# A gated cross-attention and mixture block: full-row down matmuls for the small unit, and five steps in another order

## The chip, the cores and the metric

The kernel runs on one core of a Trainium2 chip. The metric is the device time of one execution in microseconds (us). The engines are TensorE (PE in the profile; PEld are its weight loads), VectorE (DVE), ScalarE (ACT), GpSimd (POOL) and SyncE (SP), which issues the transfers.

## The reference, cut to what matters

```python
# 4 batches of 256 tokens, D = 256; per 128-wide block: scale to 448, round to fp8, scale back
x = x + tanh(g_xattn) * einsum(quant_act(layernorm(x)), quant_weight(ctx))      # per batch
h = layernorm(x)
comb = top-4 of softmax(h @ gate_w.T), made to sum to 1                         # 8 experts
moe  = sum_e comb[:, e] * ((silu(h @ wg[e].T) * (h @ wu[e].T)) @ wd[e].T)       # 176 rows each
sh   = (silu(h @ swg.T) * (h @ swu.T)) @ swd.T                                  # 704 rows
x = x + tanh(g_ffn) * (moe + sigmoid(h @ shared_gate_w.T) * sh)
```

## The kernel before, in words

**Units.** The 8 experts' 176 rows and the shared 704 make 2112 weight rows, cut into 17 units of 128 rows (`UNITS`). Units 0 to 5 of a pass are the shared part, and the last of these, position 5, has only 64 rows (`LAST`, `is_small`). Units 6 to 16 are the experts. The 1024 tokens go in two halves of 512 (batches 0 and 1, then 2 and 3), so that `n` runs from 0 to 33.

**A unit.** Products are kept near fp32 by splitting each operand into a high part, rounded to fp32r, and a low rest. ACT writes the high part of a unit's gate and up weights (`high_gu`), of its down weights (`high_d`) and of the activations (`high_a`), and applies silu (`silu_unit`). POOL writes the low parts of the weights (`low_gu`, `low_d`), DVE multiplies silu by up (`gated`), by the routing weight (`mixed`) and makes the low activations (`low_a`). PE then does `gate(n)` and `up(n)`, 6 matmuls each of 128 rows by 512 tokens, and `down(n - 2)`, 6 more (`three_passes`, L971). The small unit has gate and up side by side in one weight tile, so it has no `up`. Its down weights lie twice in 128 rows, and its activations are stacked: rows 0 to 63 of `a_hi` are the high part and rows 64 to 127 the low. For each half of the columns `down` does two matmuls for it: `d_hi` on 128 rows (L1034) and `d_lo` on 64 (L1035).

**Before the units.** Each batch goes through: variance (DVE), `centre`, `scale_x`, `mags_x` (ACT), `lift_x`, `round_x` (DVE), `transpose_xq` (PE), `copy_xqt` (ACT). Its context goes through `scale_ctx`, `mags_ctx` (ACT), `lift_ctx`, `round_ctx` (DVE). Then come `attend` (PE), `residual0` (ACT), `residual1` and `residual_sum` (DVE), the second layernorm (`stats_x1`, a power on POOL, `shift_x1` on DVE, `norm_x1` on ACT), `transpose_y2` (PE), `high_h` (ACT) and `low_h` (DVE). The block maxima of the context are transposed and spread over the partitions by two small matmuls of 8 rows (`ctx_scale_rows`, L890), which `copy_scales_ctx` reads on DVE; `scale_ctx` waits for that copy.

**Order.** Each engine works its own queue in the order in which the program text has it, with semaphores between the engines. There is no planner. Batches 0 and 1 run before the units. The steps of batches 2 and 3 are written by hand between units 0 to 16, on each engine under its own `if n == ...`. Units 0 and 1 go by batch on PE while batch 1 is still in its second norm: `gate_up_first(n, part)` does 8 matmuls with the high tokens (L1010, L1011; 256 tokens each), waits for `h_lo`, and does 4 with the low ones (L1015). Order there: units 0 and 1 on batch 0, `transpose_y2(1)`, units 0 and 1 on batch 1.

**Routing.** `router` and `transpose_logits` (PE) give the logits of a half, DVE ranks and weighs them, `transpose_comb` (PE, L964) turns the weights, `copy_comb` (ACT, L433) writes `comb_rows`, and SP sends these to DRAM and back, spread over partitions, into `mixw`; `mixed` reads it from unit 6 on.

Of the kernel before, what the change touches and what calls it, by code (L numbers as in the profile page):

```python
# [20 lines left out]
UNITS = FULL + 1  # L21
# [58 lines left out]
def flamingo_gated_block(nc, xs, ctx_t, small, w_full, w_last, comb_d, out_t):  # L80
    with ExitStack() as stack:
# [210 lines left out]
        def _(pool):  # L292
# [25 lines left out]
            def low_d(n):  # L318
                c, slot, rows = CHUNKS[n % UNITS], n % DEEP, rows_of(n)
                at = GUL if is_small(n) else GU  # L320
                pool.wait_ge(d_hi_done, n + 1)
                nc.gpsimd.tensor_tensor(d_lo[0:rows, slot, :], w_raw[0:rows, c, at:at + D],  # L322
                                        d_hi[0:rows, slot, :].bitcast(F32), ALU.subtract).then_inc(d_lo_done, 1)
# [33 lines left out]
        def _(a):  # L357
# [86 lines left out]
            def high_d(n):  # L444
                c, slot, rows = CHUNKS[n % UNITS], n % DEEP, rows_of(n)
                at = GUL if is_small(n) else GU
                rows = 2 * LAST if is_small(n) else rows
                nc.scalar.activation(d_hi[0:rows, slot, :], w_raw[0:rows, c, at:at + D], ACT.Copy).then_inc(d_hi_done, 1)  # L448
# [21 lines left out]
            high_gu(0)  # L470
# [9 lines left out]
            mags_x(1)  # L480
            residual0(0)
            high_gu(1)
            copy_xqt(1)
# [68 lines left out]
        def _(v):  # L552
# [231 lines left out]
            lifted = lift_x(0)  # L784
            round_x(0, lifted)
            lifted = lift_ctx(0)
            max_x_1 = max_x(1)
            round_ctx(0, lifted)
            scales_x(1, max_x_1)
            dequant_scales(0)  # L790
            lifted = lift_ctx(1)
            round_ctx(1, lifted)
            lifted = lift_x(1)
            round_x(1, lifted)
# [6 lines left out]
            stats_x1(1)  # L801
            low_h(0)
            shift_x1(1)
# [6 lines left out]
            for n in range(ALL):  # L810
# [68 lines left out]
        def _(pe):  # L879
# [123 lines left out]
            def gate_up_first(n, part):  # L1003
                cols = slice(part * S, (part + 1) * S)
                banks, x_of = (GATE_FIRST[n][:, cols], UP[n][:, cols]), tokens(0, part)
                pe.wait_ge(gu_lo_done, n + 1)
                pe.wait_ge(h_hi_done, part + 1)
                for which, out in enumerate(banks):
                    for k, (hi, lo) in enumerate(w_gu(n, which)):
                        nc.tensor.matmul(out, hi, x_of[k][0], start=(k == 0), stop=False)  # L1010
                        nc.tensor.matmul(out, lo, x_of[k][0], start=False, stop=False)  # L1011
                pe.wait_ge(h_lo_done, part + 1)
# [133 lines left out]
```

## Time and profile before

| | us |
|---|---|
| median of 3 runs | 185.72 (185.38 to 185.96) |
| the profiled execution, its whole time | 185.49 |
| its span | 183.5 |
| PE busy, 723 matmuls | 159.0 (87%) |
| DVE busy | 131.4 (72%) |
| ACT busy | 103.1 (56%) |
| POOL busy | 92.7 (51%) |

The busy time of an engine is the time in which the profile shows an instruction on it; that includes time in which an instruction that has begun is held back. The granted clock of PE was 1.00 of full speed in every stretch. A matmul's end is modelled; the distance between the starts of two matmuls is the surer number.

### The profile page before, as it was taken

To read this page: it belongs to the slowest core of one execution; us is meant where nothing else is said; L and a number is where in the kernel's file an instruction comes from. 1 tells how busy PE (TensorE), PEld (TensorE's weight loads), DVE (VectorE), ACT (ScalarE), POOL (GpSimd) and SP (SyncE) were. 2 spreads that over 40 slices of the span, in tenths; PEclk is the share of its full clock that TensorE was granted. 3 is DMA by queue.
4 is the path that set the end of the run, shared out by engine and by line. 5 is a ranking of instruction groups with operands and counts; after the bars stand their busy time and mean duration, and the time that the engine had idled before them with its cause. 6 is when DMAs were issued, how large, how long until landed. Compare 5 with 4: busy or idle time off the path is not lost.

```text
span 183.5 us, 2313 instructions
## 1 busy us (share of the span) xinstructions
PE 159.0 (87%) x723; PEld 122.7 (67%) x723; DVE 131.4 (72%) x265; ACT 103.1 (56%) x229; POOL 92.7 (51%) x92
## 2 busy tenths in 40 slices
PE   0022688999889999999997999999999999999992
PEld 0010357877568688777885887887886888888871
DVE  1878984897998999999866962977278455444463
ACT  2499563958546886474746764445654554443430
POOL 3120615653744468556317995556545555553450
PEclk9999999999999999999999999999999999999999
DMA  5999992000019940000000000200299400000003
GB/s 140 289 404 340 321 311 86 5 0 0 0 61 272 255 103 4 2 2 0 4 0 0 2 0 0 92 25 0 66 251 269 105 4 0 2 0 0 4 0 114
DMA packets 8049, 16.19 MB, mean 88 GB/s; under 512 B 1235, under 2 KB 1235, under 8 KB 8037
## 3 DMA queue, kind: packets, MB, share of 16 engines
q1 hardware_dynamic: 8036, 16.04, 28.9%
q8 instruction: 6, 0.10, 0.2%
q14 instruction: 7, 0.05, 0.1%
HBM read 14.95 MB, written 1.09 MB: 87 GB/s over the span
## 4 chain that ended last, share of the span: by engine, by line
PE 68%; DVE 14%; ACT 10%; issue 3%; DMA 2%; POOL 0%; DVEq 0%
PE bank L971 58%; ACT xc L380 2%; DMA x<-xs 2%; DVE act L737 2%; DVE x L660 2%; PE bank L923 2%; ACT xc L409 2%; DVE a_lo L753 1%; PE bank L1010 1%; ACT cw L372 1%; DVE bn L571 1%; ACT silu L457 1%; PE bank L1015 1%; PE bank L1011 1%; DVE amax_x L615 1%
## 5 line engine op out<-in xcount | busy, mean ns | idle before, releaser
L315 POOL TENSOR_TENSOR gu_lo<-w_raw,gu_hi 128x512 fp32r<-128x512 f32 (+1 forms) x34 | 47.5, 1398 | 21.6 <-ACT gu_hi L442 13.4
L322 POOL TENSOR_TENSOR d_lo<-w_raw,d_hi 128x256 fp32r<-128x256 f32 (+1 forms) x34 | 32.6, 960 | 44.1 <-ACT d_hi L448 44.0
L971 PE MATMUL bank<-h_hi,gu_hi 128*128 128x512 f32 x124 | 49.6, 400 | 0.5 <-ACT silu L457 0.4
L971 PE MATMUL bank<-h_hi,gu_lo 128*128 128x512 f32 x124 | 49.2, 397 | 0.0
L971 PE MATMUL bank<-h_lo,gu_hi 128*128 128x512 f32 x124 | 49.1, 396 | 0.0
L457 ACT ACTIVATE silu<-bank 128x512 f32<-128x512 f32 (+1 forms) x34 | 20.2, 594 | 45.8 <-PE bank L971 44.7
L747 DVE TENSOR_TENSOR act<-silu,mixw 128x512 f32<-128x512 f32 x18 | 14.7, 814 | 22.0 <-ACT silu L457 22.0
L753 DVE TENSOR_TENSOR a_lo<-act,a_hi 128x512 fp32r<-128x512 f32 x32 | 28.1, 877 | 0.7 <-ACT a_hi L465 0.7
L971 PEld LDWEIGHTS bank<-h_hi,gu_hi 128*128 128x128 f32 x124 | 23.3, 188 | 6.9 <-issue 1.6
L971 PEld LDWEIGHTS bank<-h_hi,gu_lo 128*128 128x128 f32 x124 | 23.3, 188 | 5.5
L971 PEld LDWEIGHTS bank<-h_lo,gu_hi 128*128 128x128 f32 x124 | 23.4, 189 | 5.2
L971 PE MATMUL bank<-a_hi,d_hi 128*128 128x512 f32 x62 | 25.2, 406 | 0.0
L971 PE MATMUL bank<-a_lo,d_hi 128*128 128x512 f32 x62 | 24.3, 392 | 0.0
L971 PE MATMUL bank<-a_hi,d_lo 128*128 128x512 f32 x62 | 24.3, 392 | 0.0
L465 ACT ACTIVATE a_hi<-act 128x512 fp32r<-128x512 f32 (+1 forms) x34 | 21.2, 623 | 5.5 <-DVE act L737 4.8
L737 DVE TENSOR_TENSOR act<-silu,bank 128x512 f32<-128x512 f32 (+1 forms) x16 | 11.0, 686 | 14.0 <-PE bank L971 10.2
L442 ACT ACTIVATE gu_hi<-w_raw 128x512 fp32r<-128x512 f32 (+1 forms) x34 | 20.8, 613 | 0.1
L308 POOL TENSOR_TENSOR rstd<-ve,minus_half 128x2 f32<-128x2 f32 x8 | 5.9, 740 | 18.9 <-DVE ve L581 18.8
L448 ACT ACTIVATE d_hi<-w_raw 128x256 fp32r<-128x256 f32 x34 | 13.8, 406 | 0.0
L971 PEld LDWEIGHTS bank<-a_hi,d_hi 128*128 128x128 f32 x62 | 11.6, 188 | 2.8 <-issue 0.3
L971 PEld LDWEIGHTS bank<-a_hi,d_lo 128*128 128x128 f32 x62 | 11.6, 188 | 2.6
L971 PEld LDWEIGHTS bank<-a_lo,d_hi 128*128 128x128 f32 x62 | 11.7, 188 | 2.4
(117 smaller groups left out, 194.8 us busy)
## 6 DMA issues: line engine op xcount, KB each, us to landing
w_raw<-w_full SPq DMA_DIRECT2D x16, 384.0 KB, 5.2
mixw<-comb_d SPq DMA_DIRECT2D x10, 256.0 KB, 5.7
x<-xs SPq DMA_DIRECT2D x4, 256.0 KB, 6.4
cw<-ctx_t SPq DMA_DIRECT2D x4, 256.0 KB, 5.8
out_t<-fin SPq DMA_DIRECT2D x4, 256.0 KB, 2.3
mixw<-comb_d SPq DMA_DIRECT2D x4, 224.0 KB, 5.6
mixw<-comb_d SPq DMA_DIRECT2D x4, 192.0 KB, 5.5
mixw<-comb_d SPq DMA_DIRECT2D x4, 160.0 KB, 4.9
```

The costliest lines, as they stand in the source:

```text
L308: nc.gpsimd.tensor_tensor(rstd[:, which, tile_slice(b)], ve[:, which, tile_slice(b)], minus_half[:, 0:BT], ALU.pow).then_inc(rstd_sem, 1)
L315: nc.gpsimd.tensor_tensor(gu_lo[:, slot, 0:cols], w_raw[:, c, 0:cols], gu_hi[:, slot, 0:cols].bitcast(F32), ALU.subtract).then_inc(gu_lo_d ...
L322: nc.gpsimd.tensor_tensor(d_lo[0:rows, slot, :], w_raw[0:rows, c, at:at + D], d_hi[0:rows, slot, :].bitcast(F32), ALU.subtract).then_inc(d ...
L380: last = nc.scalar.activation(xc[:, j, k, :], xc[:, j, k, :], ACT.Copy, scale=mul_x[:, j, k:k + 1])
L442: nc.scalar.activation(gu_hi[:, slot, 0:cols], w_raw[:, c, 0:cols], ACT.Copy).then_inc(gu_hi_done, 1)
L448: nc.scalar.activation(d_hi[0:rows, slot, :], w_raw[0:rows, c, at:at + D], ACT.Copy).then_inc(d_hi_done, 1)
L457: nc.scalar.activation(silu[0:rows, slot, :], src[0:rows, :], ACT.Silu).then_inc(silu_done, 1)
L465: nc.scalar.activation(a_hi[0:rows, slot, :], act[0:rows, slot, :], ACT.Copy).then_inc(a_hi_done, 1)
L737: nc.vector.tensor_tensor(act[0:rows, slot, :], factor[0:rows, slot, :], up, ALU.mult).then_inc(gated_done, 1)
L747: nc.vector.tensor_tensor(act[:, slot, :], factor[:, slot, :], mixw[:, c, :], ALU.mult).then_inc(mixed_done, 1)
L753: nc.vector.tensor_tensor(low, act[0:rows, slot, :], a_hi[0:rows, slot, :].bitcast(F32), ALU.subtract).then_inc(a_lo_done, 1)
L971: last = nc.tensor.matmul(out, w[k][a], x_of[k][b], start=(start and k == 0 and i == 0), stop=(stop and k == blocks - 1 and i == 2))
```

## The change

The small unit's low down weights are made on all 128 rows, and its down matmuls read all 128 rows of `d_hi`, `d_lo` and `a_hi`; the second now also adds the product of the low weights with the low activations. `high_gu(0)` and `high_gu(1)` move back on ACT. `shift_x1(1)` goes ahead of `low_h(0)` on DVE. `gate_up_first` is cut in two, `first_high` (its 8 matmuls with the high tokens) and `first_low` (its 4 with the low ones), and `transpose_y2(1)` stands between these for unit 1, batch 0. `transpose_comb` goes on PE from behind `down` of one iteration to behind the small unit's `gate` of the next, in both halves, and `copy_comb` on ACT from ahead of that unit's silu to behind it. `ctx_scale_rows(1)` goes from n = 5 to between gate(6) and up(6), and the copy of its result on DVE from n = 5 to n = 6, behind `round_x(2)`. Some names are changed and nothing else.

```diff
             def low_d(n):                                     # GpSimd
-                nc.gpsimd.tensor_tensor(d_lo[0:rows, slot, :], w_raw[0:rows, c, at:at + D], ...
+                nc.gpsimd.tensor_tensor(d_lo[:, slot, :], w_raw[:, c, at:at + D], ...
...
             mags_x(0)                                         # ScalarE
-            high_gu(0)
             scale_ctx(0)
...
             mags_x(1)
+            high_gu(0)
             residual0(0)
+            copy_xqt(1)
             high_gu(1)
-            copy_xqt(1)
             residual0(1)
...
                 if n < ALL - 2:
                     high_gu(n + 2)
-                if n == 5:
-                    copy_comb(0)
-                if n == UNITS + 5:
-                    copy_comb(1)
                 if n == ALL - 1:
                     high_a(n - 1)
                 silu_unit(n)
+                if n % UNITS == 5:
+                    copy_comb(n // UNITS)
...
             stats_x1(1)                                       # VectorE
+            shift_x1(1)
             low_h(0)
-            shift_x1(1)
...
                 if n == 5:
-                    copy_scales_ctx(1)
                     scales_x(3, max_x_3)
                     lifted_2 = lift_x(2)
                 if n == 6:
                     round_x(2, lifted_2)
+                    copy_scales_ctx(1)
...
                     if is_small(n):                           # TensorE, in down(n)
-                        nc.tensor.matmul(out[k][:], d_hi[0:2 * LAST, slot, ks], a_hi[0:2 * LAST, slot, :], ...
-                        last = nc.tensor.matmul(out[k][:], d_lo[0:rows, slot, ks], a_hi[0:rows, slot, :], ...
+                        nc.tensor.matmul(out[k][:], d_hi[:, slot, ks], a_hi[:, slot, :], ...
+                        last = nc.tensor.matmul(out[k][:], d_lo[:, slot, ks], a_hi[:, slot, :], ...
...
             keep_clock_up(2)                                  # TensorE
-            gate_up_first(0, 0)
-            gate_up_first(1, 0)
+            first_high(0, 0)
+            first_low(0, 0)
+            first_high(1, 0)
             transpose_y2(1)
-            gate_up_first(0, 1)
-            gate_up_first(1, 1)
+            first_low(1, 0)
+            first_high(0, 1)
+            first_low(0, 1)
+            first_high(1, 1)
+            first_low(1, 1)
...
                 gate(n)
                 if n == 2:
                     transpose_logits(0)
+                if n % UNITS == SHARED_UNITS - 1:
+                    transpose_comb(n // UNITS)
+                if n == 6:
+                    ctx_scale_rows(1)
                 if not is_small(n):
                     up(n)
...
-                if n == 5:
-                    ctx_scale_rows(1)
...
                 down(n - LAG)
-                if n % UNITS == SHARED_UNITS - 2:
-                    transpose_comb(n // UNITS)
```

## Rows read from the trace of the kernel before

**Rows 1.** Busy time by stretch: length, PE, PEld, DVE, ACT, POOL, clock, DMA, GB/s
```profile
64.00:86.00 22.00, 22.00 (x103) 17.36 (x103) 21.95 (x32) 14.38 (x33) 14.12 (x11) 1.00 0.10 26
86.00:100.00 14.00, 13.07 (x61) 10.21 (x59) 9.72 (x26) 8.10 (x19) 5.53 (x7) 1.00 0.00 1
```

**Rows 2.** Chain of work that ended last: start, length, what; its last long piece
```profile
139.39 39.33 PE bank L971 x168
```

**Rows 3.** PE's waits: total us, times, the longest
```profile
PE bank L890 <- DVE diag L594: 2.0, 2, 1.3
PE bank L1010 <- ACT h_hi L420: 1.1, 2, 0.8
PE bank L964 <- DVE comb L725: 0.9, 1, 0.9
```

**Rows 4.** Timeline, 0 to 20 us: start, length, instruction [idle before it]
```profile
9.84 0.17 DVE L599 COPY scl_c<-bank 128x16 f32<-128x16 f32 x1
...
10.07 0.61 ACT L442 ACTIVATE gu_hi<-w_raw 128x512 fp32r<-128x512 f32 x1
...
10.59 1.26 ACT L372 ACTIVATE cw<-cw,scl_c 128x128 f32<-128x128 f32 x4
...
12.55 0.69 DVE L604 SCALAR_TENSOR_TENSOR cw<-cm,cw 128x512 f32<-128x512 bf16 x1 [0.79 <-ACT cm L385]
```

**Rows 5.** Timeline, 20 to 36 us
```profile
25.37 0.70 POOL L308 TENSOR_TENSOR rstd<-ve,minus_half 128x2 f32<-128x2 f32 x1 [2.34 <-DVE ve L581]
...
25.86 0.69 DVE L684 TENSOR_TENSOR h_lo<-bank,h_hi 128x512 fp32r<-128x512 f32 x1 [0.57 <-ACT h_hi L420]
...
26.47 0.15 DVE L678 SCALAR_TENSOR_TENSOR shift<-mv,rstd 128x2 f32<-128x2 f32 x1
...
27.00 0.64 PE L1015 MATMUL bank<-h_lo,gu_hi 128*128 128x256 f32 x4
...
28.90 0.60 PE L923 MATMUL bank<-eye,xc 128*128 128x128 f32 x4
...
29.54 0.60 ACT L420 ACTIVATE h_hi<-bank 128x512 fp32r<-128x512 f32 x1 [1.78 <-PE bank L923]
```

**Rows 6.** Timeline, 49.4 to 66 us, without the weight loads
```profile
50.64 0.68 DVE L753 TENSOR_TENSOR a_lo<-act,a_hi 128x512 fp32r<-128x512 f32 x1
...
52.32 0.39 PE L890 MATMUL bank<-diag,ones 8*128 8x16 f32 x2 [0.73 <-DVE diag L594]
...
57.05 1.27 ACT L372 ACTIVATE cw<-cw,scl_c 128x128 f32<-128x128 f32 x4
...
57.20 0.69 DVE L737 TENSOR_TENSOR act<-silu,bank 128x512 f32<-128x512 f32 x1 [0.53 <-PE bank L971]
...
58.64 0.69 DVE L638 SCALAR_TENSOR_TENSOR xq<-xm,xc 128x512 bf16<-128x512 bf16 x1
...
59.24 1.78 DVE L747 TENSOR_TENSOR act<-act,mixw 128x512 f32<-128x512 f32 x1
...
59.91 0.60 ACT L457 ACTIVATE silu<-bank 128x512 f32<-128x512 f32 x1 [1.07 <-PE bank L971]
...
61.38 0.69 DVE L737 TENSOR_TENSOR act<-silu,bank 128x512 f32<-128x512 f32 x1 [0.35 <-PE bank L971]
```

**Rows 7.** Timeline of the full stage, 75 to 105 us
```profile
82.15 0.97 DVE L610 SCALAR_TENSOR_TENSOR cq<-cm,cw 128x512 bf16<-128x512 bf16 x1
...
83.41 0.61 PE L916 MATMUL bank<-cq,xqt 128*128 128x256 bf16 x4
...
87.49 0.69 DVE L747 TENSOR_TENSOR act<-silu,mixw 128x512 f32<-128x512 f32 x1 [0.28 <-ACT silu L457]
```

**Rows 8.** Timeline of the small unit's down, first half: first matmul, and the next unit's first
```profile
61.32 0.47 PE L1034 MATMUL bank<-a_hi,d_hi 128*128 128x512 f32 x1
...
63.00 0.50 PE L971 MATMUL bank<-h_hi,gu_hi 128*128 128x512 f32 x1
```

**Rows 9.** Groups of instructions with shapes kept apart: total us, mean ns | idle before
```profile
L322 POOL TENSOR_TENSOR d_lo<-w_raw,d_hi 128x256 fp32r<-128x256 f32 x32 | 30.5, 954 | 38.2 <-ACT d_hi L448 38.1
...
L322 POOL TENSOR_TENSOR d_lo<-w_raw,d_hi 64x256 fp32r<-64x256 f32 x2 | 2.1, 1042 | 5.9 <-ACT d_hi L448 5.9
```

More of the change, by code:

```diff
@@ L318, in low_d @@
             def low_d(n):
[L319 removed]
+                c, slot = CHUNKS[n % UNITS], n % DEEP
                 at = GUL if is_small(n) else GU
                 pool.wait_ge(d_hi_done, n + 1)
[L322 to L323 removed]
+                nc.gpsimd.tensor_tensor(d_lo[:, slot, :], w_raw[:, c, at:at + D], d_hi[:, slot, :].bitcast(F32),
+                                        ALU.subtract).then_inc(d_lo_done, 1)
             def add_shared(h, k):
@@ L444, in high_d @@
             def high_d(n):
-                c, slot, rows = CHUNKS[n % UNITS], n % DEEP, rows_of(n)
+                c, slot = CHUNKS[n % UNITS], n % DEEP
                 at = GUL if is_small(n) else GU
-                rows = 2 * LAST if is_small(n) else rows
-                nc.scalar.activation(d_hi[0:rows, slot, :], w_raw[0:rows, c, at:at + D], ACT.Copy).then_inc(d_hi_done, 1)
+                nc.scalar.activation(d_hi[:, slot, :], w_raw[:, c, at:at + D], ACT.Copy).then_inc(d_hi_done, 1)
             def silu_unit(n):
@@ L783, in _ @@
             stats(0, 1, summed_1).then_inc(var_ready, 1)
-            lifted = lift_x(0)
-            round_x(0, lifted)
-            lifted = lift_ctx(0)
+            lifted_x0 = lift_x(0)
+            round_x(0, lifted_x0)
+            lifted_c0 = lift_ctx(0)
             max_x_1 = max_x(1)
-            round_ctx(0, lifted)
+            round_ctx(0, lifted_c0)
             scales_x(1, max_x_1)
             dequant_scales(0)
[L791 to L794, printed above, removed]
+            lifted_c1 = lift_ctx(1)
+            round_ctx(1, lifted_c1)
+            lifted_x1 = lift_x(1)
+            round_x(1, lifted_x1)
             residual1(0)
@@ L1001, in up, with first_banks, first_high @@
                 three_passes(UP[n % 2][:], w_gu(n % SPLIT, 1), tokens(n // UNITS), True, True).then_inc(products_done, 1)
-            def gate_up_first(n, part):
+            def first_banks(n, part):
                 cols = slice(part * S, (part + 1) * S)
-                banks, x_of = (GATE_FIRST[n][:, cols], UP[n][:, cols]), tokens(0, part)
+                return GATE_FIRST[n][:, cols], UP[n][:, cols]
+            def first_high(n, part):
+                x_of = tokens(0, part)
                 pe.wait_ge(gu_lo_done, n + 1)
                 pe.wait_ge(h_hi_done, part + 1)
-                for which, out in enumerate(banks):
+                for which, out in enumerate(first_banks(n, part)):
                     for k, (hi, lo) in enumerate(w_gu(n, which)):
@@ L1011, in gate_up_first, with first_low @@
                         nc.tensor.matmul(out, lo, x_of[k][0], start=False, stop=False)
+            def first_low(n, part):
+                x_of = tokens(0, part)
                 pe.wait_ge(h_lo_done, part + 1)
-                for which, out in enumerate(banks):
+                for which, out in enumerate(first_banks(n, part)):
                     for k, (hi, lo) in enumerate(w_gu(n, which)):
@@ L1019, in down @@
             def down(n):
-                slot, rows, pos = n % DEEP, rows_of(n), n % UNITS
+                slot, pos = n % DEEP, n % UNITS
                 start, stop = pos in (0, SHARED_UNITS), pos in (SMALL_AT, UNITS - 1)
@@ L1033, in down @@
                     if is_small(n):
-                        nc.tensor.matmul(out[k][:], d_hi[0:2 * LAST, slot, ks], a_hi[0:2 * LAST, slot, :], start=False, stop=False)
-                        last = nc.tensor.matmul(out[k][:], d_lo[0:rows, slot, ks], a_hi[0:rows, slot, :], start=False, stop=True)
+                        nc.tensor.matmul(out[k][:], d_hi[:, slot, ks], a_hi[:, slot, :], start=False, stop=False)
+                        last = nc.tensor.matmul(out[k][:], d_lo[:, slot, ks], a_hi[:, slot, :], start=False, stop=True)
                     else:
```

## The prediction

> **What bounds the kernel now.** I read the busy shares by stage first, then TensorE's (PE's) waits, then the timeline at each place of the diff. From 64 us on PE works almost without a gap: 22.00 of 22 us between 64 and 86 us, 13.07 of 14 between 86 and 100 [rows 1], and from 139.39 us the chain of waits is 168 matmuls in 39.33 us, 0.234 us each [rows 2]. So a microsecond taken off the path before some place reaches the end, unless another engine holds it back in between. One does: VectorE (DVE) is busy 21.95 of 22 us between 64 and 86 us [rows 1]. That stage matters most here, as it lies behind nearly all the edits. Before it PE really waits at a few places, and the diff touches three: 0.8 us for h_hi, 0.9 us for comb, and (2.0 less the start-up's 1.3) 0.7 us for the context scales [rows 3].
>
> **1. Context scaled ahead of weights.** The chain at the start runs through ScalarE (ACT). high_gu(0) starts at 10.07 and the context scaling behind it at 10.59, so 0.52 us goes off ACT's queue [rows 4]. Is something else late then? The scales that scale_ctx(0) needs are copied at 9.84 + 0.17 = 10.01 us, 0.06 us ahead of the new start at 10.07. DVE stood idle 0.79 us for the magnitudes of this context before its lift at 12.55 [rows 4], so it moves by the whole 0.52 too and brings the scales and codes of batch 1 with it. high_gu(0) goes to behind mags_x(1): it delays residual0(0), which keeps its old time, while residual1(0) on DVE ends later than it. high_gu(1) goes behind copy_xqt(1), into the time in which ACT waits for PE's attention of batch 1. GpSimd (POOL) reads gu_hi(0) only after the second xq, and takes gu_lo(1) only after x1 of batch 0, so its work is not late by more than it gains. Gain 0.52; bounds 0 and 0.61 (the instruction's own length).
>
> **2. Batch 1's shift ahead of low_h(0).** The variance root of batch 1 ends at 25.37 + 0.70 = 26.07, while its shift starts at 26.47 because low_h(0) at 25.86 is in front [rows 5]. New order: shift at 26.1, normalisation 0.37 us earlier; low_h(0) starts at about 26.17 and ends at 26.86, 0.14 us before the low passes at 27.00 want it [rows 5]. By itself it gives nothing on the path, and costs nothing. If the low passes did wait, it would cost up to 0.3.
>
> **3. Batch 1's transposes between the passes.** They start at 28.90, behind four low passes (0.48 us from the chain's 0.12 a piece: 27.00 to 27.48 for the like group), and h_hi follows at 29.54; PE then stands 0.8 us [rows 3, 5]. Placed ahead of those four passes they start at 28.42, one microsecond after their input is there; h_hi moves from 29.54 to 29.07 and the four passes fill a part of PE's wait. Gain 0.47; bounds 0 and the wait of 0.8. What is late next is h_hi itself: about 0.3 us of the wait stays.
>
> So the kernel is 0.99 us ahead at 34 us. Until 49 us the path alternates between PE, the routing steps on DVE and back, all started by PE, and I let the 0.99 pass. The times below are the old ones, with this 0.99 still to be taken off.
>
> **4. Comb and scale steps later on PE.** Now gate(5) (6 matmuls, 1.4 us by rows 2) runs in the 0.9 us in which PE waited for comb [rows 3], and the transposes find comb ready. Then comes down(3), which needs a_lo(3): DVE makes it at 50.64 + 0.68 = 51.32 [rows 6]. That is a new wait of 1.0 us, where before down(3) came behind the scale matmuls at 52.32 and thus at 52.6. So PE gains 1.3 at down(3). The two scale matmuls now stand in a dense stream between gate(6) and up(6); they took 0.32 us with PE idle ahead of them, here I say 0.4. up(6) and all behind it on PE is 0.8 to 0.9 earlier, and so is gated(6), which waited for it at 57.20 [rows 6]. copy_comb goes behind silu(5): comb_rows is 0.4 later (in these times), against a broadcast that DVE reads first at 59.24; in the second half it is some 1.5 us later, by gate(22) and a silu. There the consumers on PE come two units later (over 4 us), so nothing.
>
> The other side is copy_scales_ctx(1), now behind round_x(2) on DVE, 58.64 + 0.69 = 59.3, or 58.6 with the 0.8 that gated(6) gained. ACT's scale_ctx(2) started at 57.05, and now waits until 58.6: 1.5 us. Behind it in ACT's queue stand high_gu(9) and silu(7): 58.6 + 1.2 + 0.52 gives silu(7) at 60.3 instead of 59.91 [rows 4, 6]. DVE waits for it and does gated(7) at 60.95, 0.4 before its old 61.38 [rows 6], though PE is 1.3 ahead. For this wait DVE had a cover: mixed(6) took 1.78 us at 59.24 where other such products take 0.7, until POOL's low_gu(9) was done. high_gu(9) being late, POOL is idle then and the 1.1 us are saved, to be partly lost in low_a(6), which will meet low_gu(9). I come to 0.3 us for DVE on entering its full stage, bounded by 1.3 (all that PE has) and by a loss of 1.1 (the saved collision comes back at another place). ACT's own 1.5 us of wait is no such bound, since ACT stood idle 1.07 us ahead of silu(7) [rows 6].
> The Trainium skill, page "SBUF — State Buffer", section "SBUF: two separate sides", says that VectorE with two SBUF inputs and GpSimd lock each other out for whole instructions, the first to start winning; the 1.78 us agree with it.
>
> **5. The full stage.** attend(3) on PE at 83.41 needs round_ctx(3), done at 82.15 + 0.97 = 83.12, a slack of 0.29; mixed(13) on DVE at 87.49 waited 0.28 for a silu [rows 7]. With DVE 0.3 earlier and PE more than that, this place comes 0.3 + 0.28, some 0.5 us earlier, and the rest of PE's lead (with the first small unit's saving) is lost in waiting. From here the chain of batch 3's second norm goes to 99.99 us unchanged. Term: 0.5.
>
> **6. Down matmuls of the small unit on all rows.** From 61.32 to 63.00 us four matmuls take 1.68, 0.42 each, where full ones follow at 0.234 [rows 2, 8]. Two have 64 rows and two 128, and all four are slow, so it is the change of rows that costs, some 0.19 each: 0.75 a half, and 0.1 more at the next matmul: 0.8. In the first half it falls before the full stage of DVE (nothing more than term 5). In the second half PE alone is the path: 0.8. Bounds 0 and 0.85. POOL's d_lo on 128 rows instead of 64 costs nothing: on 64 rows it took 1042 ns mean beside 954 on the full ones [rows 9].
> The Trainium skill speaks against this term: its page "TensorE: Matmul & The Clock Gate", section "Why this matters for your kernels", has a matmul of few contraction rows take the time of a full one. By it filling the rows gives nothing. Its page "TensorEngine Tiling (Array Packing)", section "Key Properties", says that a change of tiling mode drains the engine, which fits the slow pair of full matmuls. The 0.42 beside 0.234 decides for the second.
>
> **Sum.** 0.52 + 0.47 + 0.5 + 0.8 = 2.3 us. The profiled execution took 185.49 us (span 183.5 and 1.99 around it); 183.2 by it. The median shown, 185.72, is 0.23 higher: 183.4.
>
> **Rivals.**
> A. All that PE gains passes the full stage: 0.99 + 1.3 (PE's lead at gate(8), first small unit included) + 0.8 = 3.1, 182.6 us. For it: PE alone is busy to the hundredth, and POOL's collisions with DVE may fall out better. Against: DVE's 21.95 of 22 and the slack of 0.29 at attend(3).
> B. The scale wait is passed on: POOL's work behind the late high_gu(9) meets a DVE product that it did not meet before, for 1.1 us. The stage then loses 0.6 instead of gaining 0.5: 2.3 - 1.1 = 1.2, 184.5 us. For it: ACT's queue is in order, and mags_ctx(2) and scale_x(3) are behind it too.
> C. Slower than before: the wait at scale_ctx(2) makes silu(7) 0.4 late, and POOL, out of step with DVE from there on, meets its products at three more places than now, 1.1 each as at 59.24 [rows 6]: 3.7 lost against 1.8 won elsewhere (0.99 + 0.8): 187.6 us. It decides from a loss of 2.4 in this stage on. Against: DVE's collisions were there before, and some go.
> D. The slow small unit has another cause, and full rows give nothing: 1.5 left, 184.2 us. By the first of the pages on TensorE this is what would happen. For it: two of the slow matmuls already have all rows. Against: so has every fast one.
>
> **Chances.** Forecast 0.5 (its own range 182.8 to 184.0), A 0.2, B 0.15, C 0.06, D 0.09. A measurement of this kernel tells about 0.3%, 0.56 us, from no change, so faster means under 185.16. B and D may each fall short by more, and that goes to no change: faster 0.87, same 0.07, slower 0.06. Range 182.1 to 184.8: the forecast, A, and most of B and D.
>
> **What the changed profile would show.** The residual of batch 0 half a microsecond earlier (step 1); PE's wait for h_hi of batch 1 down to 0.3 (3); no wait for comb, none for diag after the start-up, a new one of about 1 us for a_lo ahead of down(3) (4); ACT idle about 2 us ahead of scale_ctx(2), released by DVE's copy; the four matmuls of the small unit at 0.23 (6); PE waiting for cq at attend(3) (5). It is wrong if PE waits there for nothing and arrives at 100 us more than 1.9 us earlier (A), or if the stage from 57 to 87 us has grown (B, C).

## The result, and the profile after

The changed kernel takes 183.36 us (median of 8, 182.62 to 184.22), the kernel before, on the same chip, 185.66 us (median of 8, 184.43 to 185.99). The ratio is 0.9889, 95% interval 0.9862 to 0.9917: 2.1 us less, between 1.5 and 2.6 (the medians are 2.3 apart). The prediction was 183.4 us. The profiled execution took 183.21 us with a span of 181.2 us: 2.3 us of each less than before.

The two traces are best laid beside each other at events that both have. I use the first high pass of batch 1 (the first gate matmul on its half of the columns, 30.28 us before, 29.34 after) as an anchor: what lies ahead of it belongs to steps 1 to 3, what lies behind it to steps 4 to 6, and a first load that lands at another moment falls out. The table's times are starts on PE in us from the span's start.

| event on PE | before | after | moved by | since the row above |
|---|---|---|---|---|
| first high pass, batch 0 | 25.98 | 25.50 | -0.48 | -0.48 |
| first high pass, batch 1 (anchor) | 30.28 | 29.34 | -0.94 | -0.46 |
| attend(2) | 74.28 | 72.01 | -2.27 | -1.33 |
| attend(3) | 83.41 | 81.87 | -1.54 | +0.73 |
| gate(16) | 99.99 | 98.45 | -1.54 | 0 |
| end of PE's long run | 178.72 | 176.41 | -2.31 | -0.77 |

The first load landed 0.05 us later in the execution after, so the first line is a gain of 0.53. The table has the whole result: 0.53 and 0.47 at the start, then 1.33 won and 0.73 lost again on the way to attend(3), and 0.77 in the second half.

**Start (steps 1 to 3).** Timeline after; columns: start, length, engine, line, operation, and in brackets the engine's idle time before it with what ended it.

```profile
9.21 0.75 DVE L568 BATCH_NORM_STATS2 bn<-x 128x6 f32<-128x256 f32 x2
...
10.12 1.26 ACT L372 ACTIVATE cw<-cw,scl_c 128x128 f32<-128x128 f32 x4
...
12.07 0.69 DVE L601 SCALAR_TENSOR_TENSOR cw<-cm,cw 128x512 f32<-128x512 bf16 x1 [0.24 <-ACT cm L385]
...
25.50 0.36 PE L1010 MATMUL bank<-h_hi,gu_hi 128*128 128x256 f32 x1 [0.35 <-ACT h_hi L420]
25.62 0.16 DVE L675 SCALAR_TENSOR_TENSOR shift<-mv,rstd 128x2 f32<-128x2 f32 x1 [0.81 <-POOL rstd L308]
...
27.97 0.60 PE L920 MATMUL bank<-eye,xc 128*128 128x128 f32 x4
28.32 0.72 PE L1018 MATMUL bank<-h_lo,gu_hi 128*128 128x256 f32 x4
...
28.60 0.60 ACT L420 ACTIVATE h_hi<-bank 128x512 fp32r<-128x512 f32 x1 [1.69 <-PE bank L920]
...
29.34 0.35 PE L1010 MATMUL bank<-h_hi,gu_hi 128*128 128x256 f32 x1 [0.30 <-ACT h_hi L420]
```

The context scaling starts at 10.12 instead of 10.59 and DVE's lift at 12.07 instead of 12.55 [rows 4]. The shift no longer stands behind low_h(0); it waits for POOL's root and nothing else. The transposes of batch 1 start at 27.97, the four low passes behind them at 28.32, where the old order had them the other way round [rows 5]; PE's wait for h_hi fell from 0.8 to 0.30.

**The middle (step 4).** Timeline after, 49 to 61 us.

```profile
48.99 0.60 PE L961 MATMUL bank<-eye,comb 128*9 128x128 f32 x4
...
50.56 0.47 PE L968 MATMUL bank<-a_hi,d_hi 128*128 128x512 f32 x1 [0.97 <-DVE a_lo L750]
...
53.52 0.39 PE L887 MATMUL bank<-diag,ones 8*128 8x16 f32 x2
...
55.62 0.69 DVE L734 TENSOR_TENSOR act<-silu,bank 128x512 f32<-128x512 f32 x1 [0.63 <-PE bank L968]
57.74 0.68 DVE L744 TENSOR_TENSOR act<-act,mixw 128x512 f32<-128x512 f32 x1
57.86 1.28 ACT L372 ACTIVATE cw<-cw,scl_c 128x128 f32<-128x128 f32 x4 [2.82 <-DVE scl_c L596]
...
59.57 0.58 ACT L456 ACTIVATE silu<-bank 128x512 f32<-128x512 f32 x1
...
59.74 1.30 POOL L315 TENSOR_TENSOR gu_lo<-w_raw,gu_hi 128x512 fp32r<-128x512 f32 x1 [3.88 <-ACT gu_hi L442]
...
60.18 0.69 DVE L734 TENSOR_TENSOR act<-silu,bank 128x512 f32<-128x512 f32 x1 [1.75 <-ACT silu L456]
...
60.79 0.81 DVE L750 TENSOR_TENSOR a_lo<-act,a_hi 128x512 fp32r<-128x512 f32 x1
```

Neither the comb transposes nor the scale matmuls wait any more (0.9 and 0.73 before [rows 3, 6]); down(3) does, 0.97 us for a_lo. The context scaling of batch 2 starts at 57.86, having waited 2.82 us for DVE's copy (57.05 before [rows 6]). The product with mixw takes 0.68 us where it took 1.78; POOL's low_gu(9), which ran beside it before, starts only at 59.74 now; and gated(7) is at 60.18 against 61.38 [rows 6].

**The full stage (step 5).** Timeline after, then the windows (columns: stretch, its length, busy us of PE, weight loads, DVE, ACT and POOL, granted clock, DMA share, GB/s).

```profile
72.01 0.61 PE L913 MATMUL bank<-cq,xqt 128*128 128x256 bf16 x4
...
72.86 0.47 PE L968 MATMUL bank<-a_hi,d_hi 128*128 128x512 f32 x1 [0.23 <-DVE a_lo L750]
...
81.10 0.67 DVE L607 SCALAR_TENSOR_TENSOR cq<-cm,cw 128x512 bf16<-128x512 bf16 x1
...
81.87 0.60 PE L913 MATMUL bank<-cq,xqt 128*128 128x256 bf16 x4
```

```profile
64.00:86.00 22.00, 21.64 (x100) 16.81 (x99) 21.39 (x36) 14.16 (x33) 16.44 (x12) 1.00 0.07 18
86.00:100.00 14.00, 13.05 (x60) 10.20 (x59) 10.06 (x21) 8.96 (x21) 5.98 (x7) 1.00 0.00 1
```

PE, which showed 22.00 of 22 us before [rows 1], now shows 21.64: it arrives 2.27 us early at attend(2), then waits 0.23 us for a_lo ahead of down(8), and reaches attend(3) when cq(3) is written (81.10 + 0.67 = 81.77), 1.54 us early. round_ctx(3) ends 1.35 us earlier than before (83.12 by [rows 7]), and of the 0.29 us that lay between its end and PE's start 0.10 is left. PE now follows DVE here at once; it was this slack that step 5 counted on. From start to start PE's two delays are longer than the one bracket says: down(8) starts 0.51 us after the matmul ahead of it, where that distance was 0.03, and attend(3) 0.52 us, where it was 0.24. These two make up the 0.73 us to within 0.03.

**The small unit (step 6).** Timeline after in the second half, and the long piece of the chain of waits behind it.

```profile
136.19 0.39 PE L1037 MATMUL bank<-a_hi,d_hi 128*128 128x512 f32 x1
136.42 0.40 PE L1038 MATMUL bank<-a_hi,d_lo 128*128 128x512 f32 x1
136.66 0.39 PE L1037 MATMUL bank<-a_hi,d_hi 128*128 128x512 f32 x1
136.89 0.39 PE L1038 MATMUL bank<-a_hi,d_lo 128*128 128x512 f32 x1
137.11 0.40 PE L968 MATMUL bank<-h_hi,gu_hi 128*128 128x512 f32 x1
```

```profile
137.28 39.13 PE bank L968 x168
```

These are PE's rows alone. The four matmuls stand 0.23 us apart (0.42 before [rows 8]), and the 168 behind them take 39.13 us (39.33 [rows 2]).

PE's waits after (columns: engine, line waited at, what for; us in total, times, longest):

```profile
PE bank L913 <- DVE cq L607: 1.8, 1, 1.8
PE bank L887 <- DVE diag L591: 1.3, 1, 1.3
PE bank L968 <- DVE a_lo L750: 1.2, 2, 1.0
```

L887 waits only at the start-up now, and comb has left the list [rows 3].

The best version that the experiments led to (b1 below) takes 181.56 us. One of its six executions lasted 555.60 us and is in no ratio.

### The profile page after: what moved, and what is told of

Its sections match the earlier page's. It is cut to its first block, busy times and chain, and to the rows that moved or that the text cites. A ratio compares the mean times of both kernels' runs of the same rounds, so it can differ in the third digit from the quotient of the medians.

```text
span 181.2 us, 2313 instructions
## 1 busy us (share of the span) xinstructions
PE 158.0 (87%) x723; PEld 122.9 (68%) x723; DVE 128.8 (71%) x265; ACT 102.9 (57%) x229; POOL 93.9 (52%) x92
## 3 DMA queue, kind: packets, MB, share of 16 engines
HBM read 14.95 MB, written 1.09 MB: 89 GB/s over the span
## 4 chain that ended last, share of the span: by engine, by line
PE 59%; DVE 18%; ACT 13%; issue 5%; DMA 2%; POOL 0%; DVEq 0%
PE bank L968 51%; ACT xc L380 3%; DVE a_lo L750 2%; DVE act L734 2%; ACT cw L372 2%; DMA x<-xs 2%; ACT silu L456 2%; DVE act L744 2%; DVE x L657 2%; PE bank L920 2%; ACT xc L409 2%; PE bank L1010 1%; DVE bn L568 1%; ACT gu_hi L442 1%; DVE amax_x L612 1%
## 5 line engine op out<-in xcount | busy, mean ns | idle before, releaser
L322 POOL TENSOR_TENSOR d_lo<-w_raw,d_hi 128x256 fp32r<-128x256 f32 x34 | 33.9, 998 | 39.6 <-ACT d_hi L447 39.5
L968 PE MATMUL bank<-h_hi,gu_hi 128*128 128x512 f32 x124 | 49.4, 398 | 0.6 <-ACT silu L456 0.4
L968 PEld LDWEIGHTS bank<-h_lo,gu_hi 128*128 128x128 f32 x124 | 23.4, 189 | 5.3
```

The lines of the kernel that those rows point to most:

```text
L322: nc.gpsimd.tensor_tensor(d_lo[:, slot, :], w_raw[:, c, at:at + D], d_hi[:, slot, :].bitcast(F32), ALU.subtract).then_inc(d_lo_done, 1)
L968: last = nc.tensor.matmul(out, w[k][a], x_of[k][b], start=(start and k == 0 and i == 0), stop=(stop and k == blocks - 1 and i == 2))
```

## The experiments

Each ratio is to the kernel before on the same chip, with its 95% interval. Positions "behind the anchor" are measured from that run's own first high pass of batch 1; before, attend(3) stands 53.13 and gate(16) 69.71 us behind it, after 52.53 and 69.11.

### e1_ctx: the kernel before with step 1 alone

```diff
             mags_x(0)
-            high_gu(0)
             scale_ctx(0)
...
             mags_x(1)
+            high_gu(0)
             residual0(0)
+            copy_xqt(1)
             high_gu(1)
-            copy_xqt(1)
```

> The kernel before with step 1 alone (context scaled ahead of weights). Theory: all of it passes, since every stage is shifted alike: the first high pass on batch 0 starts 0.5 us earlier than 25.98, gate(16) 0.5 earlier than 99.99, total -0.5 us (ratio 0.997). Rival: another input is late (scales copied 0.06 us ahead), 0 to -0.1. Rival 2: gained at the start and lost in the full stage of VectorE: at 25.98 -0.5, at 99.99 0.

Measured: 185.65 us beside 185.65, ratio 0.9987 (0.9967 to 1.0008). The first high pass of batch 0 comes 21.80 us after DVE's first instruction; before it was 22.04, after the whole change 21.51. So step 1 gave 0.24 us here, not 0.52. Timeline of e1:

```profile
9.45 0.75 DVE L571 BATCH_NORM_STATS2 bn<-x 128x6 f32<-128x256 f32 x2 [0.36 <-DMA x<-xs]
...
10.31 0.40 ACT L372 ACTIVATE cw<-cw,scl_c 128x128 f32<-128x128 f32 x1 [0.19 <-DVE scl_c L599]
```

DVE computes the moments of batch 1 ahead of the scales' copy, and in this execution batch 1's x had not landed: 0.36 us of wait go on to the copy and from it to ACT, which now waits 0.19 us. Before, ACT was busy with high_gu(0) then, and a late load cost nothing: in the trace of e4, which keeps the old order here, the moments wait 0.32 us for x and the context scaling still starts 6.65 us after DVE's first instruction, as it did before. What step 1 does give passes whole: gate(16) comes 0.25 us earlier. The gain of step 1 hangs on a load, which the prediction did not see.

### e2_y2: the kernel before with steps 2 and 3 alone

```diff
-            gate_up_first(0, 0)
-            gate_up_first(1, 0)
+            first_high(0, 0)
+            first_low(0, 0)
+            first_high(1, 0)
             transpose_y2(1)
-            gate_up_first(0, 1)
-            gate_up_first(1, 1)
+            first_low(1, 0)
+            first_high(0, 1)
+            first_low(0, 1)
+            first_high(1, 1)
+            first_low(1, 1)
```

> The kernel before with steps 2 and 3 alone (batch 1's shift first, its transposes between the passes). Theory: PE's wait for h_hi of batch 1 falls from 0.8 to 0.3 and the first high pass on batch 1 starts 0.45 earlier than 30.28; this passes to gate(16) and the end: -0.45 us (ratio 0.9975). Rival: lost in the full stage, 0 at 99.99.

Measured: 185.5 us, ratio 0.9988 (0.9967 to 1.0009). From the first high pass of batch 0 to that of batch 1 it is 30.22 - 26.39 = 3.83 us, before 4.30: 0.47 us, the figure of the term, and the wait for h_hi is 0.30. Behind that, distances are those of before. Against this stands something that has nothing to do with the edit; timeline of e2:

```profile
24.50 1.11 PE L923 MATMUL bank<-eye,xc 128*128 128x128 f32 x4 [0.16 <-ACT xc L409]
...
25.40 1.06 PE L986 MATMUL bank<-xqt,eye_b 128*128 128x512 bf16 x2
```

The four transposes take 0.90 us until the next instruction starts, where they took 0.49 in the profile of before (24.54 to 25.03): PE was still at its slower rate when they came, and the path is 0.41 us later. This differs from execution to execution: the traces of e3, e4 and a5 have it too (0.88 to 0.91 us). Steps 2 and 3 were not run apart, so that step 2 gives nothing by itself rests on the trace alone.

### e3_rows: the kernel before with step 6 alone

```diff
-                nc.gpsimd.tensor_tensor(d_lo[0:rows, slot, :], w_raw[0:rows, c, at:at + D], ...
+                nc.gpsimd.tensor_tensor(d_lo[:, slot, :], w_raw[:, c, at:at + D], ...
...
-                        nc.tensor.matmul(out[k][:], d_hi[0:2 * LAST, slot, ks], a_hi[0:2 * LAST, slot, :], ...
-                        last = nc.tensor.matmul(out[k][:], d_lo[0:rows, slot, ks], a_hi[0:rows, slot, :], ...
+                        nc.tensor.matmul(out[k][:], d_hi[:, slot, ks], a_hi[:, slot, :], ...
+                        last = nc.tensor.matmul(out[k][:], d_lo[:, slot, ks], a_hi[:, slot, :], ...
```

> The kernel before with step 6 alone (small unit's down matmuls on all rows). Theory: the four matmuls of each half start 0.23 apart; in the first half PE's 0.8 us are mostly lost in the full stage of VectorE (gate(16) 0.3 earlier than 99.99, PE waiting for the context codes at attend(3)), in the second half 0.8 reaches the end: -1.1 us (ratio 0.994). Rival A: both halves pass, -1.6. Rival D: full rows give nothing, 0.

Measured: 184.87 us, ratio 0.9955 (0.9935 to 0.9975), 0.8 us less. All four matmuls are 0.23 us apart in both halves; the rows read as those of the small unit above. Behind the anchor attend(2) is 0.78 us earlier, attend(3) 0.45, gate(16) 0.47; from 100 us on another 0.8. So of the first half's 0.78 a part of 0.3 is lost in the full stage, and 0.47 comes through; the prediction had let it bring nothing beside term 5.

### e4_comb: the kernel before with step 4 alone

```diff
-                if n == 5:
-                    copy_comb(0)
-                if n == UNITS + 5:
-                    copy_comb(1)
                 silu_unit(n)
+                if n % UNITS == 5:
+                    copy_comb(n // UNITS)
...
                 if n == 5:
-                    copy_scales_ctx(1)
...
                     round_x(2, lifted_2)
+                    copy_scales_ctx(1)
...
                 gate(n)
+                if n % UNITS == SHARED_UNITS - 1:
+                    transpose_comb(n // UNITS)
+                if n == 6:
+                    ctx_scale_rows(1)
...
-                if n == 5:
-                    ctx_scale_rows(1)
...
                 down(n - LAG)
-                if n % UNITS == SHARED_UNITS - 2:
-                    transpose_comb(n // UNITS)
```

> The kernel before with step 4 alone (comb and scale steps later on PE, comb copied after silu, scales copied after the rounding). Theory: down(3) about 1.1 earlier than 52.64 after a new wait for a_lo, up(6) 0.6 earlier, scale_ctx(2) about 1.8 later than 57.05, gate(16) 0.3 to 0.6 earlier than 99.99: -0.4 us. Rival: all of PE's lead passes, -1.0. Rival: the late scales cost, 0 or slower. If steps 1, 2-3 and 4 give 0.5, 0.45 and 0.5 here, the whole change's 1.54 us at gate(16) is their sum and the first small unit gave nothing.

Measured: 185.68 us, ratio 0.9996 (0.9975 to 1.0016). The new wait for a_lo ahead of down(3) is 0.96 us. Behind the anchor down(3) is 1.14 us earlier, attend(3) 0.41 and gate(16) 0.43. By its trace the step gives 0.4 us, as expected; its time alone cannot tell that from nothing (the interval reaches from -0.5 to +0.3 us). e3 and e4 alone give 0.47 and 0.43, and together, in the changed kernel, 0.60: gains ahead of the full stage do not add up.

### a1_copy_early: the changed kernel, scale matmuls behind down(3)

```diff
                 if n == 5:
+                    copy_scales_ctx(1)
                     scales_x(3, max_x_3)
...
                     round_x(2, lifted_2)
-                    copy_scales_ctx(1)
...
-                if n == 6:
-                    ctx_scale_rows(1)
...
                 down(n - LAG)
+                if n == 5:
+                    ctx_scale_rows(1)
```

> The changed kernel with the scale matmuls ahead of gate(6) and the scales copied at n = 5 on VectorE, so that ScalarE's wait of 2.8 us ahead of scale_ctx(2) goes. Theory: that wait was covered by the collision that mixed(6) no longer has; silu(7) comes earlier, gated(7) then waits for PE and starts at about 59.75 instead of 60.18, and the collision is back at some product: between 0.4 us faster and 0.3 slower than the change, gate(16) 98.0 to 98.7. Rival: the wait is what holds the stage: over 0.7 us faster, gate(16) under 97.8.

Measured: 183.26 us, ratio 0.9855 (0.983 to 0.9881). ACT no longer waits for the copy; attend(3) stands 52.02 us behind the anchor, 0.51 earlier than after the change, and gate(16) 68.59, 0.52 earlier. So the scale wait of step 4 was passed on in part: a half microsecond of what PE had won was held back in DVE's stage by ACT's late work. PE's wait for a_lo ahead of down(8) is gone here, and the one at attend(3) stays (0.52 us from start to start). The gain is more than the 0.4 us that I had allowed at most. It is read from the trace; the interval of the ratio overlaps that of the change (0.9862 to 0.9917).

### a2_stats_early: the changed kernel, batch 3's second statistics earlier

```diff
                 if n == 14:
-                    stats_x1(3)
                     shift_x1(3)
...
                     residual_sum(3)
+                    stats_x1(3)
```

> The changed kernel with batch 3's second variance taken at n = 13, in the 1.5 us in which VectorE waits for silu(14), instead of n = 14. Theory: the chain of batch 3's second norm sets PE's two waits (0.51 us for the normalised rows, 0.43 for silu(15)); the shift comes 3 us earlier, both waits go, and PE works through to the end: 0.9 us faster than the change, about 182.4. Rival: PE waits for something else there (h_lo of batch 3, or silu(15)), and gains 0.4 or less.

Measured: 182.81 us, ratio 0.983 (0.9806 to 0.9854). First the changed kernel at this place, then a2.

```profile
96.46 0.39 PE L968 MATMUL bank<-a_hi,d_lo 128*128 128x512 f32 x1
97.36 0.66 PE L920 MATMUL bank<-eye,xc 128*128 128x128 f32 x4 [0.51 <-ACT xc L409]
98.45 0.48 PE L968 MATMUL bank<-h_hi,gu_hi 128*128 128x512 f32 x1 [0.43 <-ACT silu L456]
```

```profile
97.28 0.39 PE L968 MATMUL bank<-a_hi,d_lo 128*128 128x512 f32 x1
97.51 0.60 PE L920 MATMUL bank<-eye,xc 128*128 128x128 f32 x4
97.86 0.48 PE L968 MATMUL bank<-h_hi,gu_hi 128*128 128x512 f32 x1
```

Both waits are gone: 0.51 + 0.43 = 0.94 us of rows. Yet the next transposes (of x1(2)) stand 70.57 us behind the anchor instead of 72.00: 1.4 us. A bracket counts from the modelled end of the instruction before (0.39 us after its start), while the next one could have started 0.23 us after it. From start to start the two places took 0.90 and 1.09 us and take 0.23 and 0.35: 0.67 + 0.74 = 1.41. So each of these two waits cost 0.2 to 0.3 us more than its bracket says. Part of what set them was a tiny instruction: the shift of batch 3 on DVE, two columns wide, took 1.23 us in the changed kernel (at 94.94 us, right behind the start of POOL's low_gu at 94.87) and 0.15 us here.

### a3_both: a1 and a2 together

> The changed kernel with both: scales copied early, batch 3's variance early. Theory: the parts add: 0.9 to 1.3 us faster than the change, 182.0 to 182.4. Rival: the waits for a_lo and for the context codes in the full stage grow by what the early copy brings, and only the 0.9 of the variance is left.

Measured: 181.94 us, ratio 0.9803 (0.9776 to 0.983). The transposes of x1(2) stand 70.12 us behind the anchor, 1.88 earlier than after the change: 0.52 + 1.4. These two do add up, since a2's waits lie behind the full stage. I had put the sum at 0.9 to 1.3 us; it is more because a2's two waits cost 1.4 us and not 0.9.

### a4_light_dve: the changed kernel with less work on DVE in the full stage

The kernel leaves out 448 of the 512 columns of five products by the routing weight, so that it computes something else; only its times are of use.

```diff
-                nc.vector.tensor_tensor(act[:, slot, :], factor[:, slot, :], mixw[:, c, :], ALU.mult)...
+                cols = 64 if 8 <= n <= 12 else HN
+                nc.vector.tensor_tensor(act[:, slot, 0:cols], factor[:, slot, 0:cols], mixw[:, c, 0:cols], ALU.mult)...
```

> The changed kernel with VectorE's products by the routing weight for units 8 to 12 on 64 of 512 columns, about 0.5 us less each; the other columns keep old values, so that part of the computation is left out. Theory: VectorE holds PE in the full stage, by the waits of 0.23 us for a_lo at down(8) and about 0.25 for the context codes at attend(3); both go, attend(3) starts at about 81.3 instead of 81.87, gate(16) 0.5 earlier than 98.45, 0.5 us faster than the change. Rival: PE alone is the bound there, 0.

Measured: 182.85 us, ratio 0.9835 (0.9811 to 0.9859). Windows of a4:

```profile
64.00:86.00 22.00, 22.00 (x103) 17.35 (x102) 20.82 (x37) 14.66 (x34) 15.17 (x12) 1.00 0.05 14
```

PE is at 22.00 of 22 us again and has no wait for a_lo ahead of down(8). attend(3) stands 51.78 us behind the anchor, 1.35 earlier than before: the whole 1.33 that PE had won by attend(2). With five products of DVE cut short the 0.73 us are not lost, so it is DVE that holds PE in this stage. At gate(16) the kernel is 0.75 us ahead of the changed one, more than the 0.5 expected.

### a5_rows64: the changed kernel, the small unit's matmuls all on 64 rows

It leaves out the low activations of these units.

```diff
-                        nc.tensor.matmul(out[k][:], d_hi[:, slot, ks], a_hi[:, slot, :], ...
-                        last = nc.tensor.matmul(out[k][:], d_lo[:, slot, ks], a_hi[:, slot, :], ...
+                        nc.tensor.matmul(out[k][:], d_hi[0:LAST, slot, ks], a_hi[0:LAST, slot, :], ...
+                        last = nc.tensor.matmul(out[k][:], d_lo[0:LAST, slot, ks], a_hi[0:LAST, slot, :], ...
```

> The changed kernel with all four down matmuls of the small unit on 64 rows (the low activations are then left out for these rows). Theory: the slowness comes from the change between 64 and 128 rows, not from 64 rows: only the first of the four and the matmul after the last are slow, the four stand 0.23 apart, and the first half's group takes about 1.1 to 1.3 us to the next unit's first matmul (1.68 before, 1.01 in the changed kernel). Rival: a matmul of 64 rows is slow by itself, all stand 0.42 apart.

Measured, in one execution: 184.29 us. Timeline of a5, second half, PE's rows:

```profile
136.66 0.40 PE L968 MATMUL bank<-h_hi,gu_lo 128*128 128x512 f32 x1
136.99 0.50 PE L1037 MATMUL bank<-a_hi,d_hi 64*128 64x512 f32 x1
137.33 0.39 PE L1038 MATMUL bank<-a_hi,d_lo 64*128 64x512 f32 x1
137.56 0.39 PE L1037 MATMUL bank<-a_hi,d_hi 64*128 64x512 f32 x1
137.79 0.39 PE L1038 MATMUL bank<-a_hi,d_lo 64*128 64x512 f32 x1
138.12 0.50 PE L968 MATMUL bank<-h_hi,gu_hi 128*128 128x512 f32 x1
138.45 0.40 PE L968 MATMUL bank<-h_lo,gu_hi 128*128 128x512 f32 x1
```

On 64 rows a matmul is as fast as on 128: 0.23 us to the next. What is slow are the two places where the number changes, each with two long distances: the first matmul on 64 rows starts 0.33 us after its forerunner and its follower 0.34 us after it, and for the first on 128 rows it is 0.33 and 0.33. Beside 0.234 each change costs 0.19 to 0.20 us in all. The old code changed four times in a group, so that the long distances of one change ran into those of the next: 137.72, 138.04, 138.46, 138.89, 139.32 and 139.66 in the kernel before are 0.32, 0.42, 0.43, 0.43 and 0.34 apart, 0.77 us over the plain distance, again 0.19 for each change. The price lies on the change.

### b1_load: a3 with batch 1's x loaded ahead of the first weights

```diff
             load_ctx(1)
-            load_w(0)
             load_x(1)
+            load_w(0)
```

> The kernel with both (scales copied early, batch 3's variance early) and the load of batch 1's x issued ahead of the first weights. Theory: step 1's gain is cut where VectorE waits for batch 1's x (0.36 us in the run of step 1 alone, 0.43 with both), since the copy of the scales is queued behind it; that wait goes, the first high pass starts 21.5 us after VectorE's first instruction as in the changed kernel's profile (21.9 with both), up to 0.4 us faster than with both, less where the load was in time anyway. Rival: the first weights, now landing later, hold something: slower.

Measured: 181.56 us (180.97 to 181.89), ratio 0.9743 (0.9707 to 0.9778). Timeline of b1:

```profile
9.05 0.73 DVE L568 BATCH_NORM_STATS2 bn<-x 128x6 f32<-128x256 f32 x2
...
10.06 1.26 ACT L372 ACTIVATE cw<-cw,scl_c 128x128 f32<-128x128 f32 x4
```

The moments wait for nothing, and the first high pass of batch 0 comes 21.50 us after DVE's first instruction, against 21.88 in a3, whose moments waited 0.43 us for x. The trace of a2 agrees: without this edit, but with x there in time, it has 21.50 as well. That closes e1's question: the missing part of step 1 is this load. The ratio is 0.6% under that of a3, some 1.1 us, where the traces show 0.38; the two were timed on different chips, and what the rest is stays open.

### b2_dummies and b3_load_dummies: more dummy matmuls ahead of the second norm

```diff
             attend(0)
+            keep_clock_up(6)
             transpose_xq(1)
```

The edit is laid over a3 for b2 and over b1 for b3.

> The kernel with both and 6 more dummy matmuls on PE, between the attention of batch 0 and the transposes of batch 1, where PE stands idle 2.8 us. Theory: in some executions the matmuls are still at the slower rate (0.43 us apart for 512 columns) at the transposes of batch 0's normalised rows (0.90 us for four instead of 0.49 in the runs of steps 2-3, of 4 and of 6 alone), which costs the path 0.4 us; with the dummies they are fast by then in every execution, and the dummies between are too: 0 to 0.4 us faster than with both, and a narrower spread. Rival: the dummies delay the transposes of batch 1 (slow ones take 2.6 us of the 2.8), up to 0.3 us slower.

> Both of the last two on top of both: if each gives its part, 0.3 to 0.7 us faster than with both (about 181.4 where that one takes 181.9); if only one does, as that one.

Measured: b2 182.67 us (180.67 to 183.16), ratio 0.9787 (0.9743 to 0.9831); b3 182.01 (180.39 to 182.83), ratio 0.9763 (0.972 to 0.9806). Neither is told from its base (0.9803 and 0.9743), and the spread is wider, not narrower as I had expected. Timeline and windows of b2:

```profile
20.27 1.67 PE L983 MATMUL bank<-xqt,eye_b 128*128 128x512 bf16 x7
...
24.22 0.66 PE L920 MATMUL bank<-eye,xc 128*128 128x128 f32 x4 [2.28 <-ACT xc L409]
```

```profile
22.00:24.20 2.20, 0.00 (x0) 0.00 (x0) 2.17 (x8) 1.09 (x2) 0.69 (x1) 1.00 0.89 296
24.20:26.00 1.80, 1.78 (x7) 0.97 (x8) 0.92 (x6) 0.92 (x3) 0.69 (x1) 0.65 0.98 354
26.00:30.00 4.00, 4.00 (x27) 4.00 (x27) 1.78 (x8) 1.20 (x3) 1.39 (x2) 0.73 0.59 222
```

(The seven matmuls of the first row are those that the kernel had already.) In this execution the extra dummies did bring PE to its fast rate early, at about 18 us: the seven old ones, which took 2.93 us in a3, now take 1.67. But they are done sooner, and PE is idle for 2.28 us ahead of the transposes. Soon behind that the granted clock falls to its lower level, 1.2 instead of 2.4 GHz: it is 0.50 in the stretch from 24.80 to 28.10 us, and the last two rows, which mix this stretch with some of full clock, show 0.65 and 0.73. The high passes, 0.12 us apart at the full clock, are 0.21 apart here, and batch 1's transposes start at 29.23 against 28.43 in a3.

In the trace of b3 the same six dummies change little:

```profile
21.21 2.64 PE L983 MATMUL bank<-xqt,eye_b 128*128 128x512 bf16 x7
```

PE turns fast within these seven, at about 23.1 us against 23.7 in a3, the idle time behind them is 0.72 us, and the clock does not fall. The other executions fit these two pictures. By the mean granted clock of each, four of b2 and three of b3 had such a fall (0.981 to 0.991; the one profiled for b2 has 0.991) and took 182.43 to 183.16 us; the other five (0.996 and more) took 180.39 to 181.58, close to b1's 180.97 to 181.89. No execution of any other kernel here is under 0.996. So the medians mix two cases, and the wider spread goes with the fall of the clock. That the longer idle time brings it about is likely from the two traces, but no run varies that time alone.

## Why the prediction was right, point by point

**Step 1, 0.52.** 0.53 in the profiled execution. The working was right for that execution only: its slack of 0.06 us between the scales' copy and ACT's new start holds when batch 1's x has landed by 9.2 us. e1 and a3 show executions in which it has not; there the term is 0.24 and 0.16 us. b1 shows it to be the load. A step that counts on 0.06 us of slack should have been followed one instruction further back in DVE's queue.

**Step 2, nothing by itself.** The shift came 0.81 us after DVE fell idle, for POOL's root, as worked out; low_h(0) ran 25.70 to 26.38, ahead of the low passes at 26.53.

**Step 3, 0.47.** 0.46 after, 0.47 in e2, and the wait left at 0.30 as said.

**Step 4, down(3) 1.3 earlier.** 1.14 measured: 52.64 to 50.56 in the change, less the 0.94 of the anchor, and 1.14 in e4. The new wait is 0.97 against 1.0. gated(6) was to be 0.8 to 0.9 earlier and is 57.20 - 55.62 - 0.94 = 0.64. scale_ctx(2) was expected at 58.6 less 0.99, which is 57.6, and came at 57.86; gated(7) at 60.95 less 0.99, which is 59.96, and came at 60.18. The saved collision is there (0.68 instead of 1.78), and low_a(6) met low_gu(9) for 0.1 us. ACT's idle time there was 2.82 us where I had said about 2. Said to be 0.3 for DVE: 61.38 - 60.18 - 0.94 gives 0.26. In the second half the later comb_rows, said to matter nowhere, makes DVE wait 0.28 us for mixw (at 133.97 us); PE does not wait for it.

**Step 5, 0.5.** 0.60 measured behind the anchor. The step's own sum, 0.3 + 0.28, is 0.58 and was rounded to 0.5. Measured, its parts are 0.41 that DVE is earlier at the end of round_ctx(3) (1.35 less the 0.94) and 0.19 of the slack. a4 shows the cause (DVE), a1 that the late copy of step 4 holds back 0.5 of it. One statement of the step was too strict: the first small unit's saving is not lost as such. Whichever gain comes first is let through to about 0.45 (e3, e4), and the second adds 0.15.

**Step 6, 0.8 in the second half.** 0.77. The rule that matmuls with few rows take full time holds in a5, and still the full rows gained, because the price was on the change of rows. The Trainium skill's page "TensorEngine Tiling (Array Packing)", section "Key Properties", has a change of tiling mode drain the engine. If the step between 64 and 128 rows is such a change, which that section does not say, a5 agrees, with 0.19 to 0.20 us at each of its two changes; the old alternation paid 0.19 at each of four, as the prediction had it.

**The sum.** 0.53 + 0.47 + 0.60 + 0.77 = 2.37, less 0.05 of later landing: the 2.3 us of the span. The four steps alone have ratios whose distances from 1 add up to 0.74% (1.4 us, each known to some 0.4 us), together 1.1%: by time alone the sum can't be tested; by traces it is 0.24 + 0.47 + 0.43 + 1.28 = 2.42. That this comes so near to 2.37 is chance: step 1 gave 0.29 less in e1, and the first halves of e3 and e4 give 0.30 more apart than together.

The nearness of 2.3 to 2.3 owes something to luck. Step 1 gives its 0.52 only when x lands early, the first small unit was left out and came through in part (0.47 alone), and by the ratio the change is worth 2.1 us, known to some 0.5.

**The rivals.** A's price was added up wrongly: with 0.8 to 0.9 from step 4 and 0.8 from the small unit PE's lead at gate(8) would be 1.6 to 1.7, not 1.3. Measured it is 1.32 all the same (63.00 - 60.74 - 0.94), since both parts came smaller: 0.65 ahead of the small unit's first matmul and 0.67 from there to gate(8). A needed PE to wait for nothing in the stage and to arrive 3.1 us early in the end; it waited 0.23 and for cq, and a4 shows what A would have needed: a lighter DVE. B and C needed the stage to grow; it shrank by 0.60, though a1 shows that B's mechanism, a scale wait passed on, was at work with 0.5 us. D fell at once with the spacing of 0.23.

## What to carry to other kernels

Lay two traces side by side from a common event, stage by stage: a gain in front of a stage that another engine fills is cut there, gains of this kind do not add up, and the next microsecond is to be had behind that stage (a2: 1.4 us by one moved line) or on the engine that fills it. Where an instruction's slack is a few hundredths, follow the queue of its producer back to the first transfer: an order that leaves no slack there turns a late load into lost time, and asking for that load earlier may be the cheaper part of the change. Keep the number of rows the same from one matmul to the next, even where half of them are not needed.

## What the runs showed of the hardware that I had not expected

- A change between 64 and 128 rows costs PE 0.19 to 0.20 us (a5: two distances of 0.32 to 0.34 us from start to start at each change instead of 0.234), and the same in alternation (0.77 us for the four changes of the kernel before).
- PE's matmuls of 512 columns stand 0.43 us apart at first and 0.22 from a turn on (b3, within the seven old dummies). The turn came between 23.4 us (a2) and 26.7 us (e3), in b2 at 17.9, and cost up to 0.4 us on the path (e2). The windows print a granted clock of 1.00 ahead of the turn too. But each trace's list of the granted clock has its first entry only at the turn (23.99 us in the kernel before, 26.34 in e2), so this 1.00 stands for no entry, and the spacing of the matmuls there is that of the lower level. For the kernel before, the clock of 1.00 in every stretch holds from 23.99 us on only. The Trainium skill's page "TensorE: Matmul & The Clock Gate", section "Seeing it yourself", warns that the clock's events in a trace were seen to be unreliable; here the entries and the spacing of the matmuls agree in all the traces.
- Dummy matmuls that end 2.28 us ahead of the work that they should serve were followed by a fall of the granted clock to half (0.50 from 24.80 to 28.10 us in b2).
- The first load lands between 3.9 us (e1: DVE's first instruction at 3.90) and 4.9 us (e3: 4.92) with no change to it, so that a profiled span can be up to 1 us off for this alone.
- A wait that a row gives as 0.51 or 0.43 us cost 0.67 and 0.74 us (a2).
- A DVE instruction two columns wide took 1.23 us beside a POOL product that had begun 0.07 us ahead of it (at 94.94 us after the change), and 0.15 us without one (a2).
